# Top-k attention stage: a depthwise product ahead of the value products, exponentials ahead of the second count

## What is computed

```python
ll   = (x1 + x2 + x3 + x4) * 0.5                 # 8 images, 64 channels, 16 x 16
high = jnp.concatenate([lh, hl, hh], axis=1)     # 192 channels, 16 x 16
# low band: 8 heads of 8 channels, 256 tokens
attn = clip(einsum('bhnd,bhmd->bhnm', q, k) * scale)     # q, k normalised
_, idx = top_k(attn, 128)                        # all but the 128 largest of a row to -1e9
out  = einsum('bhnm,bhmd->bhnd', softmax(masked attn), v)
# high bands, independent of the above
y = depthwise 3x3 conv(high)                     # then norms, silu, a 1x1 conv
```

## Time and profile before

| | us |
|---|---|
| median of 3 runs | 3963.75 |
| lowest, highest | 3952.57, 3967.2 |
| the profiled execution | 3959.45 |
| its span, first to last instruction | 3957.7 |
| of it the top-k stage, first scores to the flag (89.8 to 459.7) | 369.9 |

### The profile page before, as it was taken

One profiled execution on the slowest core, in us unless ns is written; L12 is line 12 of the kernel. 1 busy time (PEld: TensorE's weight loads), 2 busy tenths in 40 slices (PEclk: granted clock), 3 DMA queues, 4 the chain that ended last, 5 costly groups with the idle time before them and its releaser, 6 DMA issues. The chain is left out here.

```text
span 3957.7 us, 58571 instructions
## 1 busy us (share of the span) xinstructions
PE 3311.5 (84%) x22186; PEld 1315.6 (33%) x22186; DVE 3075.9 (78%) x3332; ACT 2901.6 (73%) x2954; POOL 909.0 (23%) x974
## 2 busy tenths in 40 slices
PE   3788648999999999899999999997686787786666
PEld 2455414233333333332333334433232232232212
DVE  5777666999999999579999999993376666666555
ACT  1767523999999999479999999991356665656655
POOL 1100000000000000000000000000577777777775
PEclk7666578999999999999999999998798897898677
DMA  2200000000000000000000000000213123123211
GB/s 47 103 1 1 1 0 4 1 2 2 1 1 1 2 2 1 1 1 2 1 1 1 1 2 1 2 1 16 55 53 74 53 58 74 53 62 70 58 53 43
DMA packets 117620, 89.55 MB, mean 23 GB/s; under 512 B 96496, under 2 KB 98576, under 8 KB 117340
## 3 DMA queue, kind: packets, MB, share of 16 engines
q0 software_dynamic: 28672, 58.78, 5.3%
q1 hardware_dynamic: 87036, 26.30, 3.0%
q10 hardware_dynamic: 1632, 0.56, 0.1%
HBM read 65.60 MB, written 19.96 MB: 22 GB/s over the span
## 5 line engine op out<-in xcount | busy, mean ns | idle before, releaser
L1579 ACT ACTIVATE adder_layer_Z<-adder_layer_CP,AN 128x2048 f32 x984 | 1873.3, 2005 | 31.4 <-PE PS L1540 30.5
L1540 PE MATMUL PS<-adder_layer_Z,c_adder_out 128*32 128x512 f32 x16896 | 1843.2, 593 | 57.6 <-ACT adder_layer_Z L1579 32.5
L1625 DVE TENSOR_SCALAR adder_layer_Z<-adder_layer_CP,AW 128x2048 f32 x1128 | 1369.7, 1281 | 44.8 <-PE PS L1540 30.7
L1540 PEld LDWEIGHTS PS<-adder_layer_Z,c_adder_out 128*32 128x32 f32 x16896 | 645.4, 110 | 1255.1 <-issue 1180.8
L1996 POOL DMA_INDIRECT sampler_G<-neighbours,sampler_IDX x896 | 853.4, 952 | 373.7 <-issue 272.9
L2283 ACT ACTIVATE sampler_HY<-PS,G_hat 128x512 f32<-128x512 f32 x512 | 308.9, 685 | 266.3 <-PE PS L2162 205.4
L1632 DVE SCALAR_TENSOR_TENSOR adder_layer_Z<-adder_layer_CP,AW,adder_layer_Z 128x1024 f32<-128x1024 f32 x384 | 476.4, 1282 | 33.5 <-issue 33.5
L2055 DVE TENSOR_TENSOR sampler_G<-sampler_G,PS 128x1792 f32<-128x1792 f32 x64 | 129.4, 2021 | 157.9 <-DMA sampler_G<-neighbours,sampler_IDX 152.7
L2285 ACT ACTIVATE sampler_HY<-sampler_HY 128x2048 f32<-128x2048 f32 x128 | 244.5, 1910 | 9.0 <-issue 0.4
L1497 POOL MEMSET XP<- 128x4624 f32 x1 | 4.0, 3952 | 1044.2 <-PE PS L1556 1044.2
L1492 POOL MEMSET adder_layer_CP<- 128x4624 f32 x2 | 7.9, 3954 | 1020.0 <-POOLq L1487 1019.8
(11 more groups left out here) (380 smaller groups left out, 2862.6 us busy)
## 6 DMA issues: line engine op xcount, KB each, us to landing
sampler_G<-neighbours,sampler_IDX POOLq DMA_INDIRECT x896
neighbours<-top_k_zero SPq DMA_DIRECT2D x16, 578.0 KB, 7.0
neighbours<-sampler_HT SPq DMA_DIRECT2D x256, 32.0 KB, 1.7
X<-in_x SPq DMA_DIRECT2D x8, 256.0 KB, 6.2
out<-X SPq DMA_DIRECT2D x8, 256.0 KB, 3.1
P<-in_L_conv_conv_w SPq DMA_DIRECT2D x4, 144.0 KB
P<-in_L_conv_add_w SPq DMA_DIRECT2D x4, 144.0 KB
RAW<-in_L_conv_w SPq DMA_DIRECT2D x4, 144.0 KB
```

Of the source, the lines that this page charges most:

```text
L1540: mm = t.matmul(PS[32 * j:32 * j + 32, k, :], K["adder_out"][:, 32 * i:32 * i + 32], Z[:, r % SLOTS, j, c:c + BANK], start=False, stop=Fal ...
L1579: op = a.activation(z(r, j), seen(ch, ty, tx), ACT.Relu, bias=ANf[:, weight(ty, tx, j, i)])
L1625: op = v.tensor_scalar(z(r, j), seen(ch, ty, taps[0]), AWf[:, weight(ty, taps[0], j, i)], 0.0, ALU.subtract, ALU.max)
```

## The change

TensorE's `depthwise` gets a second argument and issues one piece per call: the first piece of a step now stands between `turn(g-1)` and `values(g-1)`, the second behind `values(g-1)`. `piece_of` deals the pieces out in another way: five steps take the nine taps of one bank (2, 2, 2, 2, 1). So steps 0 to 29 have pieces, the last of every five only one, and no step holds pieces of two banks. On ScalarE `exponentials(g+1)` goes ahead of `count_aim(g+1)`. `take_depthwise` is the same, and now finds the last tap in the steps 4, 9, 14, 19, 24 and 29. The work is the same in number and size.

```diff
-            SHARE = 2
+            SPAN = 5
...
             def piece_of(g):
-                return pieces[SHARE * g:SHARE * g + SHARE]
+                first = TAPS * (g // SPAN)
+                return pieces[first + 2 * (g % SPAN):min(first + 2 * (g % SPAN) + 2, first + TAPS)]
...
-                    def depthwise(g):
+                    def depthwise(g, part):
 
-                        for s, k, tap in piece_of(g):
+                        for s, k, tap in piece_of(g)[part:part + 1]:
...
                         if g:
                             turn(g - 1)
+                        depthwise(g, 0)
+                        if g:
                             values(g - 1)
-                        depthwise(g)
+                        depthwise(g, 1)
...
                         if g + 1 < GROUPS:
+                            exponentials(g + 1)
                             count_aim(g + 1)
-                            exponentials(g + 1)
                             count_last(g + 1)
```

## The result

The changed kernel takes 3932.15 us in the median of 5 runs (3930.31 to 3936.18), the kernel before 3953.9 beside it (5 runs, 3952.36 to 3967.2). The ratio is 0.994, with a 95% interval of 0.9928 to 0.9951: 22 us or 0.6% faster, just over the bound of 0.5% that the prediction named. Forecast were 3960 and no change, with a range down to 3940 and a chance of 0.09 for a gain beyond that bound. The prediction was wrong, and its range too narrow on the lower side.

A forecast was written before the change was run, and what follows sets the result against it. TensorE was taken to bound lower-clock steps, the ScalarE-VectorE ring the others. 23 steps at 11.14 plus 6 at 10.47 make 319.0 against 322.87 us, -3.9: 3963.75 becomes 3959.9, given as 3960, range 3940 to 3972.

The forecast's parts named there:

- What bounds the kernel: Top-k stage: a mixture of steps bound by TensorE (12.41 us, lower clock) and by ScalarE and VectorE waits (9.19, higher clock).
- The ring: Scores, counts, second threshold, chosen weights, next scores through ScalarE and VectorE: 9.82 us a step before, 10.47 after.
- new step: TensorE's two-piece step at the lower clock: 2.01 + 1.82 + 1.91 + 3.43 + 1.97 = 11.14 us, against 12.41.
- the low end: TensorE's two-piece step with both pieces taken at 1.85 us: 10.96 us.
- the clock then stays at the lower level: TensorE after the change: no two pieces stand together from step 1 on, so granted clock near 0.50, below 0.62.
- clock up in part or ring-bound: Faster outcome for the stage: -8 to -39 us, chance 0.18.
- the ring-bound case: If TensorE's step is 10.47 us or less, ScalarE and VectorE bound: 29 x 10.47 = 303.6, -19 us.
- The exponentials: ScalarE's exponentials ahead of the second count: `settle` 0.92 us later; costs 0.65 a step unless TensorE's 11.14 hides it.
- The rule of the Trainium skill: Continuous TensorE work without gaps brings the full clock; the changed steps would run warm, all of them giving -39 us.
- Slower by dear switching: Lone pieces and transposes on TensorE take full row length, step 11.66 us: 0 to +8 us, 3972; chance 0.22.
- It doesn't do what it says: TensorE would have to hold the piece back though its operands are ready; left out, no chance given.
- The range: Kernel time from some 3940 us (half the steps at the higher clock) to 3972 (dear switching, on the median).

The follow-up runs named there:

- the kernel held low: Changed kernel with 4 nine-column products in place of each step's first piece, leaving out that part of the convolution: 3942.73 us, one run.
- the split kernel: Changed kernel with ScalarE's exponentials back behind the second count: 3932.76 us, ratio 0.9934 to the kernel before.
- the four small products: Changed kernel with exponentials back behind the second count and 4 nine-column products replacing each first piece, part of the convolution left out: 3936.93 us, one run.
- the kernel without pieces: All depthwise pieces left out, exponentials ahead of the second count as in the changed kernel: 3944.99 us, one run.

## Why the prediction was wrong, point by point

The 25.0 us of the 29 steps split by the runs into two parts: 322.87 to 309.67, which is the new order with the clock held at its lower level, and 309.67 to 297.85, which is the clock. The first part is a net: the kernel before had some steps at the higher clock (0.64), the kernel held low has none.

**What bounds the kernel** was right for the steps at the lower clock: TensorE comes late, and the filled hole took the wait for PT from 56.5 us to 3.5. For the steps at the higher clock it was misread. The ring doesn't set their pace: in the earlier trace rows the scores at 311.23 carry no wait, and the 9.19 us are less than the 9.82 taken for the ring. They are TensorE's own work and 2.19 us of waiting for PT. In the whole stage before, the scores waited for "chosen" four times, 10.1 us of it before the first of the 29 steps and the rest in the late steps without pieces:

```profile
PE PS L673 <- DVEq L875: 13.8, 4, 10.1
```

So the ring had three steps in which it could charge for the exponentials' move alone, and the times show no cost of it.

**The term "new step" was mis-sized: 11.14, measured 10.73**. Start to start the split kernel has 2.01 + 1.76 + 1.71 + 3.27 + 1.98. The last, from the lone piece of the earlier trace rows, was right. Transposes were taken at 1.82 (1.76), the piece in the hole at 1.91 (1.71), the values at 3.43 (3.27). The three that were too large come from rows with other neighbours: in the earlier trace rows a wait stands between transposes and values, here a piece. What makes the difference is **open**. A start that is paid behind every wait doesn't explain it: the values behind the four small products carry no wait and still take 3.41 us (189.09 to 192.50), and the lone piece of the earlier trace rows, behind a wait, took 1.97. I had added a surcharge for the change of kind, where there was one to be taken off; even the low end, 10.96, was too high. 23 x 0.41 = 9.4 us: with this term alone the sum would have been -13.3, and the run with the clock held low shows -13.2.

**The step "the clock then stays at the lower level" failed.** I had seen pairs of pieces ahead of each rise and concluded that without pairs there would be none. In the changed kernel it rises in every step, behind transposes and one piece, and TensorE needs so little time that the ring binds: -11.8 us more. The kernels with small products in the piece's place, with the same order, the same length of a step and TensorE busy for 300.25 of 304.31 and of 309.67 us, stayed at 0.50 all through, so it is the piece that brings the rise there. What ran before the rises in the trace of before was evidence that such a thing suffices, not that it is needed. I gave "clock up in part or ring-bound" 0.18, and it came about. The text had -19 for the ring-bound case (29 x 10.47); the sum measured is -25.0. Most of the rest are the 8 steps whose scores ran at the higher clock: there the ring is 0.67 shorter.

**The exponentials** were right in the mechanism and its place: the ring's 10.47 is the 10.45 of the kernel without pieces, and the last count waits for `settle` now (0.52 us in the step from 274.63, where `settle` starts 8.01 us after the scores; 8.04 were worked out). The price against the old ring was 0.33 us a step and not 0.65. What I missed is what hangs on it: undone, nothing is gained, since the clock falls to 0.56 and TensorE's 10.73 takes the ring's place in about half of the steps. There the value products run wholly or mostly at the higher clock in 11 steps of the 29 (2.1 to 2.3 us, 3.42 in the others), in the changed kernel in all. Why the same TensorE order gets 0.71 in one rhythm and 0.56 in the other is **open**. Not a lack of work explains it: TensorE is busy for 94% of the steps in the second (279.47 of 297.41) and for 76% in the first.

**The rule of the Trainium skill** ("TensorE: Matmul & The Clock Gate", Why this matters for your kernels), that continuous work brings the full clock, was set against the earlier trace rows and left as a rival. Here no run bears it out by itself: 349.32 us without a gap ran at 0.50.

**Slower by dear switching** (0.22) is out, by the 10.73. **It doesn't do what it says** is out, by the timeline.

**The range** had as its lower end half of the steps at the higher clock, -21 us. The measured gain is as large as that extreme: 21.75 us on the medians. That 3932.15 is 7.85 us below the range comes from its base: it was set on three runs of before with a median of 3963.75 and a profiled execution of 3959.45, and with two more runs the median is 3953.9. On this base -21 would be 3932.9. With the better base the time would have been near the edge of the range; the two steps above, the size of the term and the clock, would have been wrong all the same.

## What to carry to other kernels

When a step of one engine is summed from rows, take pitches (start to start) from rows that have the same neighbours as in the new order: three pitches from other neighbours hid 9 us of gain here. If the clock of TensorE decides between two bounds, give both levels their full chance: the new order gave 13.2 us with the clock held low, and the clock another 11.8. Before a step is called bound by a ring, look whether the next start carries a wait at all. And an edit on another engine that lengthens the ring can be free, and its undoing gain nothing, when the bound next to it lies within 3%: here 10.45 and 10.73.

## What the hardware showed that I had not expected

- TensorE was busy without a gap for 349.32 us at a granted clock of 0.50, running scores, transposes and products of nine columns, with one product of 512 columns in 23 of the 29 steps.
- The same instruction order on TensorE ran at a mean clock of 0.71 and of 0.56, depending only on where ScalarE runs one activation.
- These two traces, whose clock differs by 0.15, have sums of 29 steps that differ by 0.44 us (297.85 and 297.41).
